# Row fetches of a graph kernel: byte offsets instead of row numbers, sixteen register values a load, 61 tiles instead of 44

## What is computed

```python
edge_index = jnp.stack([src, dst])
xn = _layernorm(x, axis=-1)
x = x + _L0_gnn_ref(xn, edge_index, edge_weight, W, b) + _L0_mix_ref(xn[None], Wq, Wkv, Wproj, bproj)[0]
x = x + _L0_ffn_ref(_layernorm(x, axis=-1)[None], Wg, bg, bias, W1, b1, W2, b2)[0]
# _L0_gnn_ref
HW = H @ W
msgs = edge_vals[:, None] * HW[col]
return jax.ops.segment_sum(msgs, row, num_segments=N_NODES) + b
```

## Time and profile before

| | us |
|---|---|
| three runs | 3811.88, 3810.78, 3808.42 |
| median | 3810.78 |
| the profiled execution | 3811.51 |
| its span, from the first to the last instruction | 3809.8 |
| busy in it: PE, DVE, POOL, ACT | 2769.5, 2526.5, 2461.2, 635.4 |

### The profile page before, as it was taken

One profiled execution on the slowest core, in us unless ns is written; L12 is line 12 of the kernel. 1 busy time (PEld: TensorE's weight loads), 2 busy tenths in 40 slices (PEclk: granted clock), 3 DMA queues, 4 the chain that ended last, 5 costly groups with the idle time before them and its releaser, 6 DMA issues. The chain is left out here.

```text
span 3809.8 us, 70900 instructions
## 1 busy us (share of the span) xinstructions
PE 2769.5 (73%) x16407; PEld 2275.1 (60%) x16408; DVE 2526.5 (66%) x6338; ACT 635.4 (17%) x1335; POOL 2461.2 (65%) x2387
## 2 busy tenths in 40 slices
PE   1457676577777776667666777666654999999998
PEld 1346666366556565555555555555432888888887
DVE  8999998355555555777777777777683544454444
ACT  8212222311111110000000000000032221122221
POOL 0047777477777777777777777777717378744444
PEclk9988778789999999998889888998877999999999
DMA  5957775644444444444444444444382455544443
GB/s 174 303 165 233 227 220 156 205 121 125 127 127 124 127 124 128 130 131 127 129 130 130 130 130 131 131 125 129 112 251 105 78 119 121 111 79 72 72 72 56
DMA packets 357535, 522.47 MB, mean 137 GB/s; under 512 B 59192, under 2 KB 278332, under 8 KB 357180
## 3 DMA queue, kind: packets, MB, share of 16 engines
q0 software_dynamic: 128832, 269.87, 28.1%
q1 hardware_dynamic: 172947, 191.01, 16.6%
q10 hardware_dynamic: 55401, 57.82, 4.9%
HBM read 378.21 MB, written 140.28 MB: 136 GB/s over the span
## 5 line engine op out<-in xcount | busy, mean ns | idle before, releaser
L757 POOL DMA_INDIRECT message<-h_table,records x1616 | 1552.3, 961 | 526.0 <-issue 508.1
L1258 PE MATMUL bank<-message,select 128*128 128x256 f32 x3232 | 925.6, 436 | 593.7 <-issue 306.9
L1258 PEld LDWEIGHTS bank<-message,select 128*128 128x128 f32 x3232 | 666.3, 215 | 811.1 <-issue 420.9
L1815 DVE TENSOR_SCALAR select<-iota_n,records 128x128 f32<-128x128 f32 x1660 | 595.7, 359 | 513.8 <-PE bank L1258 483.9
L1823 DVE TENSOR_TENSOR acc<-acc,bank 128x256 f32 x1660 | 683.0, 411 | 9.6 <-PE bank L1258 6.3
L801 POOL DMA_INDIRECT out<-acc,row_of x224 | 350.9, 1566 | 359.3 <-DVE acc L2235 234.8
L718 POOL DMA_INDIRECT lists<-placed,dest_i x300 | 351.0, 1170 | 316.3 <-ACT placed L934 222.6
L1498 PE MATMUL bank<-w,acc 128*128 x1792 | 407.6, 381 | 8.1 <-DVE acc L2219 7.8
L1485 PE MATMUL bank<-fx_t,acc 128*128 128x256 f32 x1792 | 408.1, 381 | 1.6 <-ACT fx_t L1078 1.6
L1485 PEld LDWEIGHTS bank<-fx_t,acc 128*128 128x128 f32 x1792 | 342.3, 191 | 49.2 <-issue 2.1
L1498 PEld LDWEIGHTS bank<-w,acc 128*128 128x128 f32 x1792 | 333.0, 191 | 51.1 <-issue 10.0
(11 more groups left out here) (315 smaller groups left out, 3405.0 us busy)
## 6 DMA issues: line engine op xcount, KB each, us to landing
fetched<-h_table SPq DMA_DIRECT2D x3200, 1.0 KB
fetched<-h_table ACTq DMA_DIRECT2D x2432, 1.0 KB
rows<-block_dram SPq DMA_DIRECT2D x75, 514.5 KB
acc<-x_sorted SPq DMA_DIRECT2D x112, 260.0 KB, 2.8
message<-h_table,records POOLq DMA_INDIRECT x1616
xt_in<-xt_dram SPq DMA_DIRECT2D x98, 256.0 KB
x_sorted<-blank_rows ACTq DMA_DIRECT2D x42, 390.0 KB
lists<-zeros_list SPq DMA_DIRECT2D x8, 1664.0 KB, 15.2
```

The costliest lines, as they stand in the source:

```text
L757: pool.indirect_dma_start(out=message[:, k % SETS, j, :], out_offset=None, in_=h_table, in_offset=Offset(ap=records[:, k * SET + j, 0:1], ...
L1258: last = nc.tensor.matmul(ps, select[:, slot % 2, j, :], rows_of, start=True, stop=True)
L1815: return V.tensor_scalar(select[:, k % 2, j, :], iota_n[:, :], records[:, k * SET + j, 1:2].bitcast(F32), records[:, k * SET + j, 2:3].bit ...
```

## The change

The values in `fetch_row` are no longer row numbers but byte offsets: VectorE multiplies by 1024 where it converted. The DMA takes 1024 bytes at that offset out of `h_table` seen as bytes. A batch is sixteen rows, with sixteen registers. SyncE fetches a tile in every 12 sets (33 tiles, sets 27 to 411), ScalarE in every 14 (28 tiles, sets 36 to 414), 61 together. In the context stage ScalarE issues the rows of a unit's first set between the K part and the V part of `split_k`, those of the other two behind it.

```diff
-    SP_SPAN, SP_SET = 16, 27
-    ACT_SPAN, ACT_SET = 20, 37
+    SP_SPAN, SP_SET = 12, 27
+    ACT_SPAN, ACT_SET = 14, 36
...
+        ROW_BYTES = 4 * C
+        h_bytes = h_table.rearrange("n c -> (n c)").bitcast(U8)
...
-            for a in range(first, end, 8):
-                n = min(8, end - a)
-                rows_at = load_offsets(eng, registers[0:n], fetch_row[at:at + 1, :], a, n, NB * P - 1)
+            for a in range(first, end, 16):
+                n = min(16, end - a)
+                byte_at = load_offsets(eng, registers[0:n], fetch_row[at:at + 1, :], a, n, (NB * P - 1) * ROW_BYTES)
                 for j in range(n):
-                    eng.dma_start(fetched[a + j:a + j + 1, queue, i % 2, :], h_table[ds(rows_at[j], 1), :]).then_inc(s_fetched[queue][i % 2], 16)
+                    eng.dma_start(fetched[a + j:a + j + 1, queue, i % 2, :].bitcast(U8),
+                                  h_bytes[ds(byte_at[j], ROW_BYTES)].unsqueeze(0)).then_inc(s_fetched[queue][i % 2], 16)
...
-            def split_k(unit, first=False):
+            def split_k(unit, between, first=False):
...
                 act.activation(relu_kq[:, :], bank[4][:, :], ACT.Relu).then_inc(s_k_split, 1)
+                between()
                 act.wait_ge(s_v_psum, unit + 1)
...
             for unit in range(PAIRS):
-                split_k(unit, first=unit == 0)
-                if unit == 0:
-                    act.wait_ge(s_fetch_row, 1)
-                fetch_ahead(CONTEXT_FIRST + unit * CONTEXT_SETS, CONTEXT_FIRST + (unit + 1) * CONTEXT_SETS)
+                first_set = CONTEXT_FIRST + unit * CONTEXT_SETS
+
+                def first_rows():
+                    if unit == 0:
+                        act.wait_ge(s_fetch_row, 1)
+                    fetch_ahead(first_set, first_set + 1)
+                split_k(unit, first_rows, first=unit == 0)
+                fetch_ahead(first_set + 1, first_set + CONTEXT_SETS)
...
-            V.tensor_copy(fetch_row[:, :], bank[6][0:FETCHED, 0:P]).then_inc(s_fetch_row, 1)
+            V.tensor_scalar(fetch_row[:, :], bank[6][0:FETCHED, 0:P], float(ROW_BYTES), None, ALU.mult).then_inc(s_fetch_row, 1)
```

More of the change, by code:

```diff
@@ L54, in gps_layer @@
     from concourse import mybir
-    F32, BF16, I32 = mybir.dt.float32, mybir.dt.bfloat16, mybir.dt.int32
+    F32, BF16, I32, U8 = mybir.dt.float32, mybir.dt.bfloat16, mybir.dt.int32, mybir.dt.uint8
     ALU, ACT, AX = mybir.AluOpType, mybir.ActivationFunctionType, mybir.AxisListType.X
@@ L575, in bring_x @@
                     sp.dma_start(x_in[:, pair % 2, :, :], x_pairs[pair:pair + 1, :, :, :].rearrange("a p u c -> p (a u) c")).then_inc(s_x_in[pair % 2], 16)
-            row_registers = [sp.alloc_register(f"row_{i}") for i in range(8)]
+            row_registers = [sp.alloc_register(f"row_{i}") for i in range(16)]
             def fetch_ahead(first, end):
@@ L1008, in _ @@
             act.wait_ge(s_late, 2)
-            row_registers = [act.alloc_register(f"row_{i}") for i in range(8)]
+            row_registers = [act.alloc_register(f"row_{i}") for i in range(16)]
             def fetch_ahead(first, end):
```

## The result

The changed kernel takes 4060.75 us (median of six runs, 4058.72 to 4064.01), the kernel before 3808.46 (six runs beside them): a ratio of 1.0662, 95% interval 1.0648 to 1.0676. It is 6.6% slower; 4092 had been forecast, in a range of 3785 to 4150. The profiled execution took 4058.72 us, its span is 4057.0, so 247.2 us more than before.

What follows compares the result with a forecast made beforehand. GpSimd's gathers were taken as the bound, at 1.263 us each, with both fetching queues nearly full. From 3811.5 us, -21.5 (gathers) + 88 (ScalarE, context) + 214 (SyncE, mix) = +280 gave 4092 us; range 3785 to 4150.

Steps and rivals of the forecast that it cites:

- the 21.5 us that the removed gathers promised: GpSimd: 17 gathers fewer at 1.263 us each, 21.5 us saved if GpSimd stays the bound.
- the cheap load: Rival, chance 0.28: a register load of 16 costs 1.4 to 1.5 us wherever it starts; 3790 to 3799 us in all.
- eight values' cost: Rival, chance 0.10: a load of 16 off a multiple of 4 costs 2.05 us, as eight values do; some 3910 us.
- the one with the address instruction left: Rival, chance 0.07: a register instruction per row stays on SyncE and ScalarE, a copy replacing the product; some 4380 us.
- The slack of 5 us: Context stage: only some 5 us of ScalarE's 93 us excess is hidden before VectorE and TensorE wait, leaving +88.
- the 357 us for twelve units: SyncE, mix stage: loads 111, rows 212, around the loads 24, inputs 10; sum 357 us, or 29.8 a unit.
- The lead of 56 us: Mix stage: SyncE's rows land 39 us before use, plus 19 from longer spans, less landing; hides 56 of 270 us.
- The signs named: Loads near 1.4 and 3.7 us by start, no address instruction, gather gaps ending with TensorE, fetched-tile matmuls waiting, stages near 810 and 1400.

## Why the prediction was right

**Bound and mechanism: right.** The single-row queues took the bound from GpSimd, through loads of 16 that start off a multiple of 4. Rounding the starts gives all of the loss back, and 20 of the 21.5 us that the removed gathers promised; at the old spans the other parts move nothing. The range says less: from 3785 to 4150 it took in the cheap load too, so the load prices and the stage lengths bear the mechanism out, and not the time alone.

**Prices: right, SyncE's a little high.** Off a multiple of 4, 3.75 us had been taken for 16 values; the medians are 3.64 (SyncE) and 3.76 (ScalarE). The working given for it doesn't make 3.75: 1.006 + 13 x 0.224 is 3.92, and from the lower start, 2.012, it is 3.62; the value taken lies between. On a multiple of 4, 1.4 and 1.5; they are 1.24 and 1.27. A row was taken at 0.331 and 0.324; it takes 0.322 and 0.325. The rival of the cheap load, which had 0.28, falls on the off-start price, and so does that of eight values' cost (3.6, not 2.05); the one with the address instruction left falls because no such instruction is in the trace. The Trainium skill's Runtime: NRT & Kernel Launch (Instruction fetch mechanics) has about 200 ns per register for loads in the launch: these off-start loads agree, with 0.200 us a value. The Trainium skill's DMA: Bandwidth & Descriptors (Latency and other measured facts) gives a register load a floor of about 600 ns. It isn't one here: one value took 505 ns on SyncE, and VectorE's loads of four 342.

**ScalarE in the context stage:** 16.5 us a unit forecast, 16.43 measured. The stage was to grow by (16.5 - 14.7) x 49 - 5 = 83 us; it grew by 68.3. A unit grew by 1.65, since before it stood at 14.78 and not 14.7: -7. The slack of 5 us was right (1.65 x 48 = 79 became 73.7 up to the last unit). Another 5.4 us came back behind the last unit, in the four sets of weights: at the last K projection 12 gathered tiles stood unused, against 3 before.

**SyncE in the mix stage: two errors that cancel.** The unit was forecast at 29.8 and lasts 28.97: of the 357 us for twelve units ten weren't there, 2.0 in the dear loads, 2.6 in the good ones, 5.8 in 640 rows. So the growth up to the last unit is (28.97 - 24.53) x 48 = 213 us, not (29.8 - 24.6) x 48 = 250. The lead of 56 us was the step that failed: from the first Q projection to the last unit's it is 1372.9 us (2955.4 - 1582.5) against 1178.6 (2695.0 - 1516.4), so 194.3 of the 213 are left and only 19 were hidden. The first five units still run at 25.2 us ((1708.3 - 1582.5) / 5), and then the lead is used up. The issues of the first and the sixth unit's transposed input show it (timeline of SP):

```profile
1561.28 0.36 SPq L567 DMA_DIRECT2D xt_in<-xt_dram  x1
...
1703.97 0.36 SPq L567 DMA_DIRECT2D xt_in<-xt_dram  x1
```

The first goes out 21.2 us ahead of its Q projection (1582.5), the sixth 4.3 (1708.3), and from the fifth on none more than 4.3; in the kernel before it is 24 to 32 us all along. The difference, some 18 us, is the lead that was there. The forecast had reckoned it from a tile's last row to its use; but SyncE also brings each unit's input, which TensorE needs at the next unit's first set, and that, not the fetched tile, is late first. 37 us too much and 37 too little: +194 forecast (250 - 56), +194.3 measured. That this term came out is luck.

**What was left out:** in the last eleven sets no input is needed, 15 gathered tiles stand unused at the last Q projection (3 before), and 12.7 us come back. With the 15 us of the context stage this is most of the 33 us between 4092 and 4059.

**The signs named:** stage lengths near 810 and 1400 us (809.8 and 1375.9), the loads and the missing product were as described. Two were not. No matmul on the fetched tile waits for a DMA. And the gaps ahead of the gathers go under "issue" (703.3 us), with only 14.7 under TensorE; what gives them away is the longest of them, 10.6 us where the rounded version shows 0.3, and the full ring behind them.

## What to carry to other kernels

Before a list is spread more finely over a queue, look at where its pieces start: a price seen at one alignment is not the price at another, and here one rounding turned 6.6% slower into 0.5% faster. Lead is measured at the first thing that is late in a queue, so go through everything that the queue carries, the loads for other stages too. A helper that is 95% occupied has no room for a third more work until its price per piece has fallen by a quarter, and in every place, not only in the median.

## What the runs showed of the hardware

A register load from a start at a multiple of 4 brings four values in about the time of one: 16 values take 1.19 us there and 3.50 elsewhere, 8 values 0.75 and 1.90. A start off by one loses all of it, also for the full groups inside the load: 16 values from an odd start cost 16 times 0.2 beside a fixed 0.3. And a register instruction of 37 ns costs 87 ns of SyncE's time between two row DMAs, and 66 of ScalarE's (0.391 against 0.325 us).

The window of 1620 to 2600 us in the changed kernel (length; busy us and instructions of PE, PEld, DVE, ACT and POOL; granted clock; DMA share; GB/s):

```profile
1620.00:2600.00 980.00, 614.03 (x2216) 479.03 (x2215) 632.31 (x1571) 36.90 (x68) 641.09 (x669) 0.84 0.38 112
```

TensorE's granted clock is a mean of 0.84 of 2.4 GHz here, made of stretches at 2.4 and at 1.2, and 0.90 before in the same window. The Q projections, most of them right behind a wait, take 634 ns in the median where they took 379. That the waits pulled the mean down isn't shown: with the starts rounded, where those waits are gone, it is 0.88, under 0.90 too. Nor is it shown that the clock cost time; in this stretch SyncE set the pace.
